# Last layer of an adjacency stack: another order of the units and of the operations on each, and distances as products over 128 rows

## The reference

```python
deg = jnp.maximum(adj.sum(axis=1, keepdims=True), 1e-08)
w = adj / deg
log_ij = _logmap(x[:, None, :], x[None, :, :], c)   # for every pair of nodes
agg = jnp.einsum('ij,ijc->ic', w, log_ij)
transformed = agg @ weight + bias
return _expmap(jnp.zeros_like(transformed), transformed, c)
```

## Time and profile before

| | |
|---|---|
| median of three runs | 1583.29 us |
| the profiled execution | 1582.32 us, span 1580.5 us |
| mean granted TensorE clock | 0.940 |
| TensorE busy | 1392.8 us (88%) |
| VectorE busy | 1235.0 us (78%) |
| ScalarE busy | 930.4 us (59%) |
| GpSimd busy | 213.2 us (13%) |

### The profile page before, as it was taken

How to read it: one execution, slowest core, us unless ns; L and a number is a source line. 1 busy time by engine, 2 the same in 40 slices (tenths; PEclk the granted TensorE clock), 3 DMA queues, 4 the chain that set the end, 5 groups by cost and what they waited for, 6 DMA issues and landing times. The chain is left out here.

```text
span 1580.5 us, 20433 instructions
## 1 busy us (share of the span) xinstructions
PE 1392.8 (88%) x7857; PEld 603.8 (38%) x7882; DVE 1235.0 (78%) x1623; ACT 930.4 (59%) x888; POOL 213.2 (13%) x145
## 2 busy tenths in 40 slices
PE   4999999789978699999999999979988898888870
PEld 1433333223324244454454454534433333333330
DVE  4899866676785877968969958528688878999877
ACT  0000286358633555445456456766879989989964
POOL 1000000000000000000000001223224444444430
PEclk9999999999997799999999999989869989999995
DMA  9999599979999255434434432234534546455600
GB/s 332 409 409 409 233 407 410 413 286 409 409 414 411 76 189 216 179 134 181 180 120 180 184 117 67 79 108 158 176 103 137 179 150 204 148 181 179 213 15 27
DMA packets 135896, 348.93 MB, mean 221 GB/s; under 512 B 7732, under 2 KB 57208, under 8 KB 135544
## 3 DMA queue, kind: packets, MB, share of 16 engines
q1 hardware_dynamic: 119968, 329.27, 56.0%
q10 hardware_dynamic: 15832, 18.36, 3.3%
HBM read 329.78 MB, written 17.83 MB: 220 GB/s over the span
## 5 line engine op out<-in xcount | busy, mean ns | idle before, releaser
L955 PE MATMUL ps<-ring,X 128*64 128x512 f32 x512 | 263.8, 597 | 15.2 <-DVE ring L2149 15.2
L956 PE MATMUL ps<-work,X 128*64 128x512 f32 x512 | 263.8, 597 | 0.0
L1471 ACT ACTIVATE work<-ring 128x2048 f32<-128x2048 f32 x64 | 122.3, 1911 | 156.4 <-PE ps L963 122.9
L963 PE MATMUL ps<-work 128*64 128x512 bf16 x768 | 208.2, 380 | 0.0
L961 PE MATMUL ps<-work 128*64 128x512 bf16 x768 | 208.2, 380 | 0.0
L727 POOL TENSOR_TENSOR ring<-ring,work 128x1024 f32<-128x1024 f32 x72 | 170.8, 2372 | 247.7 <-DVE work L2406 247.7
L824 PE MATMUL ps<-ring,work 128*64 128x512 f32 x672 | 159.5, 620 | 20.7 <-DMA ring<-in_adjT 20.7
L720 POOL TENSOR_SCALAR work<-ring 128x1024 int16<-128x1024 uint8 x24 | 27.0, 1127 | 1031.8 <-DMA ring<-codes 930.7
L961 PEld LDWEIGHTS ps<-work 128*64 128x64 bf16 x768 | 84.7, 110 | 177.4 <-issue 151.9
L1131 PE MATMUL ps<-ident,work 128*128 128x128 f32 x448 | 79.8, 305 | 52.5 <-DVE work L2338 26.0
L1297 ACT ACTIVATE work<-work,code_bias 128x2048 uint8<-128x2048 bf16 (+1 forms) x32 | 62.3, 1947 | 90.6 <-DVE work L1892 80.2
(11 more groups left out here) (365 smaller groups left out, 2847.2 us busy)
## 6 DMA issues: line engine op xcount, KB each, us to landing
ring<-in_adjT SPq DMA_DIRECT2D x88, 2048.0 KB, 15.9
work<-in_adjT SPq DMA_DIRECT2D x28, 2048.0 KB, 20.0
ring<-in_adjT SPq DMA_DIRECT2D x24, 1024.0 KB, 9.7
ring<-in_adjT SPq DMA_DIRECT2D x48, 512.0 KB, 3.8
ring<-codes SPq DMA_DIRECT2D x32, 512.0 KB, 3.7
ring<-in_adjT SPq DMA_DIRECT2D x64, 256.0 KB, 3.0
codes<-work ACTq DMA_DIRECT2D x32, 256.0 KB, 6.1
codes<-work ACTq DMA_DIRECT2D x64, 128.0 KB, 1.8
```

What stands on the lines that cost most here:

```text
L955: nc.tensor.matmul(ps[0:F, h, :], rows, ring[:, r, k, cols], start=start, stop=stop)
L956: nc.tensor.matmul(ps[F:P, h, :], rows, negs[:, pair, i, cols], start=start, stop=stop)
L963: mm = nc.tensor.matmul(ps[F:P, 2 + h, :], part, less[:, pair, i, cols], start=start and t == 0, stop=stop and t == 2)
L1471: nc.scalar.activation(negs[:, pair], ring[:, s % RING, 2 * pair:2 * pair + 2, :], ACT.Relu, scale=-1.0).then_inc(negs_made, 1)
```

## The change

Order of units: by target quarter (first quarter 1, then 0, 2, 3), all kinds of a quarter in one string, all sums in bank 4. The turn: both halves in one go, into banks 6 and 5, in period n+1; both reads by VectorE behind the sum, one period earlier than before. VectorE's order in a period: g(n-1), adds of sums, product(n+1), sum(n), both `mirror_weights`(n-1). ScalarE's: Ln(n), Ln(angle)(n-1), Relu(n+1), Exp(+)(n), Exp(-)(n). TensorE's: distances(n+1), gather(n-2), mirror products, turn(n-1), push(n+1). The push waits for the product, since the product now reads the distances from PSUM in place of one of its two reads of `u.log`. The distances are products over all 128 rows, where both halves hold the same values, with half the scale. `move_x` runs in one piece of 8 through bank 6, at periods 15, 16, 19 and 20; the flips are turned at periods 4 and 9 (before 2 and 10).

```diff
@@ -216,8 +216,8 @@
-        ORDERS = ["OOODOODODOODIIOODOOD", "OOOODIDIOOODODOOOO", "OOOODIDIOOOOOOOO", "OOOODIDIOOOOOOOODD"]
+        ORDERS = [(1, "OOODOODODOODII"), (0, "DDIIDD"), (2, "OOOOOOOODIDIOOOODOOOOD"), (3, "OOOOOOOODIDIOOOOOOOOOOOOOOOODD")]
...
+        units, turned_units = [], []
+        for I, order in ORDERS:
...
+                u.first, u.last = i == 0, i == len(order) - 1
...
-        FLIP_AT, FLIPS_OUT_AT = (26, 2, 10), (28, 3, 10)
+        FLIP_AT, FLIPS_OUT_AT = (26, 4, 9), (28, 5, 10)
+        MOVES_AT = [u.n + 1 for u in units if u.kind == "D" and u.n > LAST_AT + 4][0:NQ]
@@ -1086,51 +1070,50 @@
                 nodes = VT[:, u.I * QC:(u.I + 1) * QC]
                 for h, b in enumerate(u.rows):
                     mm = nc.tensor.matmul(ps[:, u.banks + h, :].rearrange("p (t c) -> p t c", t=2),
-                                          UT[h * F:(h + 1) * F, b * P:(b + 1) * P],
-                                          u.columns(nodes[h * F:(h + 1) * F, :], h), start=True, stop=True)
+                                          UT[:, b * P:(b + 1) * P], u.columns(nodes, h), start=True, stop=True)
                 mm.then_inc(dist_ready, 1)
 
             def push_apart(u):
 
                 if u.first:
                     pe.wait_ge(signs_copied, FLIPPED[u.I])
-                pe.wait_ge(raised, u.n + 1)
+                pe.wait_ge(prod_made, u.n + 1)
                 for h, k in enumerate(u.blocks):
                     mm = nc.tensor.matmul(ps[:, u.banks + h, :].rearrange("p (t c) -> p t c", t=2),
                                           signs_w[u.J][:, k * P:(k + 1) * P], u.columns(signs_m[u.I], h),
                                           start=False, stop=True, skip_group_check=True)
                 mm.then_inc(far_added, 1)
 
-            def move_x(n, blocks):
-
-                bank = 5 if n else 7
-                if n:
-                    pe.wait_ge(direct_added, [u.n for u in ends].index(MOVED_AT[n] - 3) + 1)
-                else:
-                    pe.wait_ge(sum2_read, NQ)
-                if n >= 2:
-                    wait_for_copies(COPIED[n])
-                for c in blocks:
+            def move_x(n):
+
+                pe.wait_ge(mirror_weighted, 2 * sum(u.turned for u in units[0:MOVES_AT[n]]))
+                if n == 0:
+                    wait_for_copies(COPIED[3])
+                for c in range(CB):
                     b = n * CB + c
-                    mm = nc.tensor.matmul(ps[:, bank, c * F:(c + 1) * F], UT[0:F, b * P:(b + 1) * P], w3_sb[:],
+                    mm = nc.tensor.matmul(ps[:, 6, c * F:(c + 1) * F], UT[0:F, b * P:(b + 1) * P], w3_sb[:],
                                           start=True, stop=True)
-                if CB - 1 in blocks:
-                    mm.then_inc(moved_made, 1)
-
-            def turn_g(u, h):
-
-                if h == 0:
-                    pe.wait_ge(g_made, u.n + 1)
-                if u.offs or h:
-                    pe.wait_ge(mirror_weighted, 2 * u.offs + h)
-                else:
-                    pe.wait_ge(sum2_copied, 2 * NQ)
-                if h == 0 and u.offs == FLIP_TURNS:
-                    pe.wait_ge(signs_copied, FLIPPED[3])
-                for c in range(GB):
-                    mm = nc.tensor.transpose(ps[:, 6, c * P:(c + 1) * P],
-                                             u.angle[:, (h * GB + c) * P:(h * GB + c + 1) * P], ident[:])
-                mm.then_inc(g_turned, 1)
+                mm.then_inc(moved_made, 1)
+
+            def turn_g(u):
+
+                pe.wait_ge(g_made, u.n + 1)
+                moves = sum(n <= u.n for n in MOVES_AT)
...
@@ -1183,36 +1163,31 @@
                     turn_flips(0)
                 if i == SLOTS - 3:
                     distances(units[0])
+            push_apart(units[0])
             for n in range(LAST_PERIOD):
-                if unit_at(n):
-                    push_apart(units[n])
                 if unit_at(n + 1):
                     distances(units[n + 1])
-                if n - 1 in MOVED_AT:
-                    move_x(MOVED_AT.index(n - 1), range(GB, CB))
-                if n == FLIP_AT[2]:
-                    turn_flips(2)
-                if turned_at(n - 2):
-                    turn_g(units[n - 2], 1)
                 if unit_at(n - 2):
                     gather(units[n - 2])
                 for quad, c in products[n]:
                     mirror_products(quad, c)
                 if turned_at(n - 1):
-                    turn_g(units[n - 1], 0)
-                if n in MOVED_AT:
-                    move_x(MOVED_AT.index(n), range(GB))
+                    turn_g(units[n - 1])
+                if unit_at(n + 1):
+                    push_apart(units[n + 1])
+                if n in MOVES_AT:
+                    move_x(MOVES_AT.index(n))
                 if n in (LAST_AT, LAST_AT + 2):
                     turn_last_nodes((n - LAST_AT) // 2)
-                if n == FLIP_AT[1]:
-                    turn_flips(1)
+                if n in FLIP_AT[1:]:
+                    turn_flips(FLIP_AT.index(n))
...
@@ -1522,7 +1497,7 @@
-                    ins = nc.scalar.activation(UT[h * F:(h + 1) * F, cols], banks[0:F], ACT.Copy, scale=-2.0 * DIST_SCALE)
+                    ins = nc.scalar.activation(UT[h * F:(h + 1) * F, cols], banks[0:F], ACT.Copy, scale=-DIST_SCALE)
                 ins.then_inc(ut_copied, 1)
@@ -1610,15 +1585,16 @@
 
             raise_dist(units[0])
             for n in range(LAST_PERIOD):
-                v = unit_at(n - 1)
-                if v:
-                    act.wait_ge(sum_made, v.n + 1)
-                    nc.scalar.activation(v.angle, v.angle, ACT.Ln, scale=2.0 / DIST_SCALE).then_inc(
-                        angle_made, 1)
-                u = unit_at(n)
+                u, v = unit_at(n), unit_at(n - 1)
                 if u:
                     act.wait_ge(prod_made, u.n + 1)
                     nc.scalar.activation(u.log, u.log, ACT.Ln, bias=TINY_PROD, scale=1.0).then_inc(log_made, 1)
+                if v:
+                    act.wait_ge(sum_made, v.n + 1)
+                    nc.scalar.activation(v.angle, v.angle, ACT.Ln, scale=2.0 / DIST_SCALE).then_inc(angle_made, 1)
+                if unit_at(n + 1):
+                    raise_dist(units[n + 1])
+                if u:
                     if u.n >= 3:
                         act.wait_ge(weighted, u.n - 2)
                         w = units[u.n - 3]
...
@@ -1802,7 +1774,7 @@
             def read_att_weights():
                 dve.wait_ge(gat_ready, 1)
                 V.tensor_copy(spread[:, F:2 * F], ps[:, 4, F:2 * F])
-                V.tensor_copy(w3_sb[:], ps[0:F, 4, 2 * F:3 * F])
+                V.tensor_scalar(w3_sb[:], ps[0:F, 4, 2 * F:3 * F], 2.0, None, ALU.mult)
@@ -2325,7 +2297,8 @@
             def multiply(u):
 
                 dve.wait_ge(raised, u.n + 1)
-                V.scalar_tensor_tensor(u.log, u.log, DIST_SCALE, u.log, ALU.add, ALU.mult).then_inc(prod_made, 1)
+                V.scalar_tensor_tensor(u.log, ps[:, u.banks:u.banks + 2, :].rearrange("p h c -> p (h c)"),
+                                       0.5 * DIST_SCALE, u.log, ALU.add, ALU.mult).then_inc(prod_made, 1)
 
             def mirror_weights(u, h):
 
@@ -2335,7 +2308,7 @@
                     if u.quad >= 2:
                         dve.wait_ge(mirrored, u.quad - 1)
                 few = h if u.off else 0
-                V.tensor_tensor(folded[u.quad % 2][few][:, :, u.cols[h]], ps[:, 6, :].rearrange("p (b c) -> p b c", c=P),
+                V.tensor_tensor(folded[u.quad % 2][few][:, :, u.cols[h]], ps[:, 6 - h, :].rearrange("p (b c) -> p b c", c=P),
                                 strip(u.quad)[:, few * GB:(few + 1) * GB, u.cols[h]], ALU.mult).then_inc(mirror_weighted, 1)
 
             sums_added = [0, 0]
...
@@ -2393,19 +2366,19 @@
 
             multiply(units[0])
             for n in range(LAST_PERIOD):
-                v = unit_at(n - 3)
-                if v and v.last:
-                    add_direct(v)
-                if n - 1 in products_end[:-1]:
-                    quad = products_end.index(n - 1)
-                    add_mirror(quad, units[quad_ends[quad]])
                 v = unit_at(n - 1)
                 if v:
                     dve.wait_ge(angle_made, v.n + 1)
                     dve.wait_ge(inv_made, v.n + 1)
                     V.scalar_tensor_tensor(v.angle, v.angle, ANGLE_CLIP, v.log, ALU.min, ALU.mult).then_inc(g_made, 1)
-                if turned_at(n - 2):
-                    mirror_weights(units[n - 2], 0)
+                w = unit_at(n - 2)
+                if w and w.last:
+                    add_direct(w)
+                if n - 1 in products_end[:-1]:
+                    quad = products_end.index(n - 1)
+                    add_mirror(quad, units[quad_ends[quad]])
+                if unit_at(n + 1):
+                    multiply(units[n + 1])
                 u = unit_at(n)
                 if u:
```

(34 more changed lines are left out.)

81 lines of the change are left out of this document (36 added, 45 removed).

## The result

The changed kernel takes 1617.09 us in the median (1613.71 to 1618.44, four runs), the kernel before, run beside it, 1584.09 (1582.99 to 1585.11, four runs). The ratio is 1.0204, with a 95% interval of 1.0188 to 1.022: **slower by 2.0%, 33 us**. The forecast was 1593 in 1574 to 1606, so the sign was right and the size was not: over three times the forecast loss, outside the range. A second series gave 1619.56 and 1.0238 (1.0202 to 1.0275).

The account below looks back on a forecast made before the run. The prediction took a 5.25 us loop over ScalarE and VectorE as the bound, with TensorE outside it. It added 6.1 us for units 12 to 71 and 4.4 for the earlier part to 1582.3, giving 1593, range 1574 to 1606.

Parts of the forecast that it names:

- The loop distances, Relu, product, sum: Last layer after the change: these four steps, one after the other, take 5.38 us a period for every unit.
- the loop of 5.25: Quiet periods before the change: Exp(+), sum, turning product, product, Ln over ScalarE and VectorE, 5.25 us, to be cut.
- Exp(+) of unit 0: Start of the last layer: it waits behind Relu of unit 1 and its longer distances, +3.4 us, at 1125.0.
- Fourfold products: Periods 13 and 14: four products each bring TensorE to 6.30 us, costing 1.8 us in all.
- The moves: Moves of x at periods 15, 16, 19, 20: 0.77 us over the loop except at 19, 2.3 us in all.
- Adds of sums: Quarter changes: gathers wait for an add that is a period old, with three fewer adds; costs nothing.
- Units 0 to 12: First twelve periods: 81.7 us against 84.3 at full clock, plus two half-clock spells of 3.5 us each.
- The tail: Behind unit 71, to the kernel's end: nothing changes, 0 us.
- Rival B: TensorE becomes the bound at half clock, with four more spells of 4 us: 1609 us; chance 0.13.
- A: Rival: the clock stays full and small steps hide in the loop's slack, 1577 us, or 1570; chance 0.22.
- C: Rival: full products cost TensorE no more than the pair, ScalarE's order bounds the kernel, 1555 us; chance 0.03.
- D: Rival: VectorE's product still collides with GpSimd, +1 us a period, 1650 us; chance 0.02.

Follow-up runs that it names:

- e3: Changed kernel with the moves of x run behind the gather of their period instead of behind the push: 1612.99 us, ratio 1.0209 to the kernel before.
- e7: Changed kernel with the flips of the last two quarters turned into PSUM bank 7 instead of 6: 1616.49 us, ratio 1.0215 to the kernel before.
- e8: Changed kernel, full distances, with moves behind gather, direct adds behind sum, early decayed and fold products ahead of turn and push, flips in bank 7: 1605.07 us.
- e1: Changed kernel with its distances again as pairs of 64-row products: 1573.81 us, ratio 0.9947 to the kernel before.
- e2: Kernel before with only the full 128-row distances added: 1586.00 us, ratio 1.0027 to the kernel before.
- e9: Changed kernel with distances as pairs of 64-row products, each pair issued twice: 1620.89 us, ratio 1.0243 to the kernel before.
- e4: Changed kernel with VectorE's product reading SBUF twice instead of PSUM once: 1706.19 us, ratio 1.0797 to the kernel before.
- e5: Changed kernel with distances as 64-row pairs, moves behind the gather and direct sums added behind the sum: 1574.58 us, ratio 0.9957 to the kernel before.
- e6: e5 with the last decayed product and layer 2's fold ahead of turn and push, and flips in bank 7: 1571.10 us, ratio 0.9933 to the kernel before.
- e10: e6 with the distance pairs of units 17 to 20 issued twice: 1570.43 us, ratio 0.9921 to the kernel before.

## Why the prediction was right in its sign and wrong in its size

**Right.** The loop distances, Relu, product, sum was named, and replaced the loop of 5.25. Relu waits for the distances and the distances for the sum. The product takes 1.22 to 1.23 us from PSUM where it took 1.22 from SBUF: no cost of the bank, as taken from the rows.

**Right by luck.** Exp(+) of unit 0 was forecast at 1125.0 and came at 1125.28, but the first distances were not counted as longer, which costs 0.76 us by the second ones (6.19 behind the first instead of 5.43), and in this execution the layer began 0.43 earlier; in the second series that Exp(+) came at 1129.66. Fourfold products cost 1.9 us (forecast 1.8), but in three periods (13 to 15: 0.42, 0.72 and 0.72) and not in two.

**Signs of being wrong.** From unit 12 to 71 TensorE is busy 93% and its granted clock 0.98, where over 95% and 1.0 were forecast. What the prediction called proof of an error did appear: the half-clock spells are more than four (in windows of 5 us the granted clock is 0.80 near 1130, 0.66 near 1157, 0.61 near 1170, 0.82 near 1185, 0.50 near 1207, 0.65 near 1265, 0.75 near 1370, 0.82 near 1400 and 0.86 near 1557).

**Wrong, term by term.** The span grew by 34.9 us where 10.5 was forecast; the 24.4 between are these:

1. *The loop, 5.38 against 5.49: 0.11 x 59 = 6.5 us.* The term at fault is distances to Relu, 1.93 put together from a two-record product over 65 rows; four records take 1.98 and Relu starts at 2.02. The other steps were off by 0.01 at most. In this loop a tenth of a microsecond is 0.4% of the kernel's time.
2. *The moves, 2.3 against 9.2: 6.9 us.* I added up TensorE's work in that period and compared it with the loop, as if it could run beside it. The change's own order puts the move between the push, which waits for the product, and the next distances, so all of it is in the loop. The sum to make was 2.02 + 1.06 + 1.23 + 0.53 + 1.92 = 6.8, which is what two of the four took. That is 1.33 over the loop, 5.3 of the 9.2 us; 0.56 is the add in period 16, and 3.35 the half clock in period 20, the one move that I had put at nothing because no products stand in its period. e3 has 5.6 us back in these periods. The fall isn't bound to the move: in e7, with the move where it was and the same 1.45 us idle ahead of it, the clock stayed at 1.00 and period 20 took 6.88.
3. *Adds of sums, "nothing": 2.1 us; two half-clock falls, none forecast behind unit 12: 2.0 us.* I had written that the add is a period old. It waits for the gather of its own period and stands ahead of the product: 0.56 in period 22, 1.52 in 44, where that gather ran at half clock (in e8, with the add behind the sum, both take 5.49). The falls are in periods 38 and 43. Small steps take 1.7 (1 forecast), and the last period is 1.7 shorter: net 3.1. The fall of period 38, TensorE in the changed kernel:

```profile
1366.70 0.60 PE L1082 MATMUL ps<-X,mid_w 2*128 2x512 bf16 x2 [1.37 <-DVE turn_in L2300]
...
1367.83 3.50 PE L1072 MATMUL ps<-work 128*128 128x512 f32 x4 [0.53 <-DVE work L2386]
```

   A unit without a turn leaves TensorE idle until the product is there, and the distances behind take 3.50 instead of 1.98 (granted clock 1.00 from 1361 to 1366, 0.51 from 1368 to 1371).
4. *Units 0 to 12, +1.0 forecast beside the later start, +6.4 measured: 5.4 and 0.3.* I counted two spells at half clock. There are five, and the sign copies hold the turn for 3.58 us, twice. I had priced them as 2 us of ScalarE's time each, and named one idle stretch of TensorE there (2.7 us) as a cause of half clock, but not as a wait that holds push and distances of the next unit.
5. *The tail, put at nothing: 2.1 us.* In the new order g of the last units comes later beside Exp(+), TensorE idles for it (3.29 us), and the last gathers meet a half clock (0.50 from 1558.9 to 1561) and take 1.97 us instead of 1.08. The changed kernel's rows:

```profile
1556.57 2.35 POOL L712 TENSOR_TENSOR ring<-ring,work 128x1024 f32<-128x1024 f32 x1 [3.10 <-DVE work L2373]
...
1558.97 1.97 PE L1134 MATMUL ps<-ring,work 128*64 128x256 f32 x8 [3.29 <-POOL ring L712]
```

Behind 2, 3 and 5 is one mistake. I priced the loop well and then asked of each further step whether its engine had room, as in the kernel before, where TensorE is in no loop. With distances in the loop, TensorE's program order is part of it: whatever stands between product and distances counts in full, and so does a fall of the clock. The full distances at half clock take 3.6 us (3.50, 3.63 and 3.78 in the rows above), 1.6 more in the loop; in the kernel before the granted clock is lower still (0.96 in the mean of units 12 to 71, against 0.98), and most of its periods still take 5.25. Rival B, at 1609 and 0.13, named such falls and is nearest in its number, but they aren't most of the loss: behind unit 12 the half clock accounts for 3.35, 1.5, 0.5 and 1.0 us in periods 20, 38, 43 and 44, 6.3 of the 22.7.

**The rivals.** A (faster, 1577) fell, C (full products cost no more) fell by e1, e2 and e9. D didn't happen, but was underpriced: I took 1 us a period from the earlier trace rows and said 1650 (71 periods would even then have given 1664); in e4 units 12 to 71 take 420.5 instead of 339.1 us, 1.4 a period, and the kernel 1706. And six products of the kernel before take over 1.8 us, not the five that I had counted.

**What stays open.** Why the clock falls at one idle stretch and not at a like one beside it isn't settled: of e5, e6 and e10 the places could be shown, not foretold. That e1, e5, e6 and e10 all take 300.8 to 300.9 us for units 12 to 71 looks like a law and is a sum: in e5 and e6 period 21 gives back what the other moves gain (periods 16 to 22 take 42.8 us in e1 and 43.0 in both), and in e10 they take 39.6, but the later ones 3.3 us more. Whether falls that are moved must come back is not shown. Why units 0 to 12 took 90.7 us in one execution and 93.0 in another of the same kernel stays open too.

## What to carry to other kernels

When a reordering cuts one loop, write out the next one in program order of every engine in it, and price each piece of work that stands between two of its steps in full, the rare ones (a move, an add at a quarter's end) as well; "its engine has room" holds only for engines outside the loop. Test a bundle's parts alone and together: here −0.5% and +0.3% made +2.0%, and the part to leave out was the one that looked nearly free in the old kernel. And take the length of an operation that enters the loop from a row with the same number of records, since an error of 0.1 us comes back in each period.

## What the runs showed of the hardware

- Two 64-row f32 products of 512 columns on the two halves of the rows run side by side: 1.13 us for the pair (four records), against 1.98 for the 128-row form (four records) and 1.99 for the pair issued twice (eight).
- A VectorE product with two SBUF inputs that starts while GpSimd is in an elementwise call ended 1.07 to 1.11 us after GpSimd did (55 of 55 calls in e4, 24 of 25 in the kernel before), so it took 2.75 us instead of 1.22 at 1582.36 in e4. Where it started 0.14 to 0.17 us first, GpSimd's call took 3.27 to 3.32 instead of 2.37 us (five calls in e4). With one input from PSUM it kept to 1.21 to 1.23 in all 72 calls of the changed kernel, 60 of which start while GpSimd is at work.
- The granted clock fell to half within a stretch in which TensorE had been idle for no more than 1.37 and 0.53 us at a time (ahead of 1367.83 in the changed kernel, where the distances took 3.50 us; 1.00 from 1361 to 1366, 0.51 from 1368 to 1371), and doubling four short pairs of products kept it at 1.00 (1244 to 1256 in e10) in a place where it had fallen to 0.50 (from about 1249 us in e6).
